# Squares of the L1 keys summed on GpSimd, self attention in packed rows, and a woven opening

## The reference, cut to what matters

```python
# layer 0, cross attention
q_in = x @ Wq + lora(x); k_in = org_ctx @ Wk + lora(org_ctx); v_in = org_ctx @ Wv + lora(org_ctx)
out = attention(q_in, k_in, v_in) + attention(q_in, ipa_ctx @ Wk_ipa, ipa_ctx @ Wv_ipa)
# layer 1, cross attention: K is normed over all 256 values of a key, before the heads are split
K = l2norm(key @ Wk + bk); V = value @ Wv + bv; Q = l2norm(query @ Wq + bq)
# layer 1, self attention: 16 heads of 16 values, 256 tokens in each of 2 batches
q = rope(x @ w_q.T); k = rope(x @ w_k.T); v = x @ w_v.T
y = softmax(q k.T / sqrt(16)) v;  return y @ w_o.T
```

## Time and profile before

| | us |
|---|---|
| median of 3 runs | 2178.71 (2175.78 to 2178.97) |
| the profiled execution | 2177.05 |
| its span, first to last instruction | 2175.3 |
| PE busy | 1946.5 (89%) |
| DVE busy | 1110.6 (51%) |
| ACT busy | 1031.1 (47%) |
| POOL busy | 627.5 (29%) |

### The profile page before, as it was taken

The page is one execution under the profiler, slowest core; times in us unless marked ns, Lnnn a source line. Parts: engine busy times, 40 slices in busy tenths (PEclk is TensorE's granted clock), DMA queues, the critical chain, the costliest instruction groups (busy, mean ns, idle before and its releaser), DMA issues. The chain is left out here.

```text
span 2175.3 us, 33966 instructions
## 1 busy us (share of the span) xinstructions
PE 1946.5 (89%) x13716; PEld 1323.1 (61%) x13716; DVE 1110.6 (51%) x1572; ACT 1031.1 (47%) x1395; POOL 627.5 (29%) x298
## 2 busy tenths in 40 slices
PE   5689999999899999999999666768998899687998
PEld 2466766667566676766666444457446644466787
DVE  2378676675666758676540543256004400465665
ACT  1144444444444444444441421036996699232443
POOL 1006555464544646555473030010000000100000
PEclk9799999999999999999999786979999999898999
DMA  5230000000300000000020100114552355200221
GB/s 183 63 112 6 6 11 6 16 6 6 93 1 15 6 6 16 6 13 4 1 77 1 58 1 1 32 49 88 85 91 61 76 94 83 78 1 1 88 88 39
DMA packets 89862, 90.60 MB, mean 42 GB/s; under 512 B 29896, under 2 KB 79760, under 8 KB 86384
## 3 DMA queue, kind: packets, MB, share of 16 engines
q1 hardware_dynamic: 86848, 85.97, 16.3%
q10 hardware_dynamic: 2864, 2.51, 0.4%
HBM read 58.57 MB, written 8.91 MB: 31 GB/s over the span
## 5 line engine op out<-in xcount | busy, mean ns | idle before, releaser
L744 POOL TENSOR_TENSOR sums<-sums,probs 128x1024 f32<-128x1024 f32 x224 | 534.8, 2388 | 355.1 <-ACT probs L777 305.4
L828 DVE TENSOR_REDUCE part_max<-psum_banks 128x2 f32<-128x1024 f32 (+1 forms) x256 | 312.6, 1224 | 125.7 <-PE psum_banks L990 121.2
L777 ACT ACTIVATE probs<-psum_banks 128x1024 f32<-128x1024 f32 x240 | 245.7, 1024 | 123.2 <-PE psum_banks L1036 116.1
L1050 PE MATMUL psum_banks<-probs,values 128*64 128x256 f32 x2048 | 278.4, 393 | 0.3 <-ACT probs L780 0.3
L755 ACT ACTIVATE keys<-psum_banks 64x512 fp32r<-64x512 f32 x256 | 151.5, 592 | 243.7 <-PE psum_banks L963 240.5
L2434 ACT ACTIVATE probs<-psum_banks,k_inv_norm 128x1024 f32<-128x1024 f32 x256 | 257.7, 1215 | 1.3 <-PE psum_banks L2449 1.2
L821 DVE TENSOR_TENSOR keys<-psum_banks,keys 64x512 fp32r<-64x512 f32 x256 | 176.3, 689 | 121.6 <-ACT keys L755 115.5
L1050 PEld LDWEIGHTS psum_banks<-probs,values 128*64 128x64 f32 x2048 | 124.5, 136 | 99.7 <-issue 60.0
L1018 PEld LDWEIGHTS psum_banks<-q_hi,keys 128*128 128x128 f32 x1024 | 138.1, 189 | 76.7 <-issue 51.7
L1018 PE MATMUL psum_banks<-q_hi,keys 128*128 128x256 f32 x1024 | 184.7, 303 | 0.0
L760 ACT ACTIVATE values<-psum_banks 128x512 f32<-128x512 f32 x128 | 76.5, 598 | 193.1 <-PE psum_banks L975 193.1
(11 more groups left out here) (436 smaller groups left out, 3159.6 us busy)
## 6 DMA issues: line engine op xcount, KB each, us to landing
k_pairs<-keys SPq DMA_DIRECT2D x192, 128.0 KB, 4.3
ctx_tok<-in_ctx SPq DMA_DIRECT2D x16, 384.0 KB, 3.4
wk_pair<-wkv_parts SPq DMA_DIRECT2D x16, 256.0 KB, 2.9
wv_quad<-wkv_parts SPq DMA_DIRECT2D x8, 512.0 KB, 3.7
w_gate_up<-in_L_ffn_gate_proj_w SPq DMA_DIRECT2D x8, 512.0 KB, 3.9
w_gate_up<-in_L_ffn_up_proj_w SPq DMA_DIRECT2D x8, 512.0 KB, 4.8
w_down<-in_L_ffn_down_proj_w SPq DMA_DIRECT2D x8, 512.0 KB, 5.7
ctx_tok_b<-in_ctx SPq DMA_DIRECT2D x8, 384.0 KB, 4.4
```

The costliest lines, as they stand in the source:

```text
L744: pool.tensor_tensor(sums[:, :, :, :], probs[:, 0, :, :, :] if step == 1 else sums[:, :, :, :], probs[:, step % SLOTS, :, :, :], ALU.add). ...
L777: act.activation(probs[:, step % SLOTS, :, :, :], scores, ACT.Exp, scale=SCALE0).then_inc(p_ready, 1)
L828: dve.tensor_reduce(part_max[:, :, i, c], psum[:, bank:bank + 2, 0:width], AX, ALU.max).then_inc(m_read, 1)
L1050: last = pe.matmul(psum[rows(h), 3, 0:L], values[:, kt, at:at + HD0], probs[:, step % SLOTS, h, j, :], start=kt == 0, stop=kt == KT - 1, t ...
```

## The change

Three parts.

1. `l1x_keys_values`: for each chunk GpSimd adds the second half of the squares to the first, and `sum_squares` has one product for each group of tokens instead of two; it waits for GpSimd's semaphore.
2. `l1_self_attention`: after the rotation q and k are split into high and low fp32r parts, which are laid out in rows of 64 (q: high, high, low, zero; k: high, low, high, one), so that two heads fill 128 rows; they are turned in four rounds of 16 transposes. First q k is computed with queries in the partitions for the maxima (16 `top` items, each a tile of queries and four heads); the negative maxima are turned (2 `turn` items) and copied by SP into the fourth row group of the queries, 8 DMAs a batch. Then k q is computed with keys in the partitions (16 `exp` items), exponentiated in one ACT instruction of 1024 elements, and weighed without a transpose of the probabilities.
3. The opening: `setup` issues the 20 weight loads before it waits for `x`; the ipa loads are issued in `l0_queries`; the ipa chain and the 8 context steps share one block; the first `wk_pair` and `wv_quad` are loaded in it.

```diff
 def setup(core, meanwhile):
                 sp.dma_start(core.x[:, :, :], ...).then_inc(x_in, 16)
+                meanwhile(sp)
                 sp.wait_ge(x_in, 16)
 def l0_queries(core, wq, xnT, qT, last, tokens):
             def _(sp):
+                for dst, src in last.pairs:
+                    sp.dma_start(dst, src).then_inc(last.arrived, 16)
                 for step in range(tokens.SLOTS):
                     tokens.start(sp, step)
+class FirstWeights:
+    def load_keys(self, sp, m):
+        sp.dma_start(self.wk_p[:, m % 2, :, :].bitcast(F32),
+                     self.w_parts[0, :, :, m % PAIRS * P:(m % PAIRS + 1) * P]).then_inc(self.wk_in[m % 2], 16)
+    def load_values(self, sp, quad): ...
+def l0_last_weights_and_context(core, last, qT, p_ipaT, parts_stored, first_w, tokens, started, cA_hi, cA_lo, cB):
+            def _(sp):
                 sp.wait_ge(parts_stored, 32)
+                first_w.load_keys(sp, 0)
+                first_w.load_values(sp, 0)
+                first_w.load_keys(sp, 1)
+                for i in range(started, STEPS_C):
+                    if i >= SLOTS:
+                        sp.wait_ge(turned, i - SLOTS + 1)
+                    tokens.start(sp, i)
+            def _(pe):
+                def turn(i):
+                    pe.wait_ge(tokens.arrived[i % SLOTS], 32 * (i // SLOTS + 1))
+                    if i >= 2:
+                        pe.wait_ge(hi_ready, 2 * (i - 1))
+                        pe.wait_ge(lo_ready, 2 * (i - 1))
+                    turn_tokens(pe, core, 2 * (i % 2), tokens.tok[:, i % SLOTS, :, :]).then_inc(turned, 1)
                 ... # transposes of the ipa tokens
+                turn(0)
                 ... # 16 products with 8 columns
+                turn(1)
+                pe.wait_ge(k_ready, 4)
                 for b in range(B):
                     ... # 8 score products of batch b
+                    turn(2 + b)
                 ... # transposes of the scores
+                for i in range(4, STEPS_C - 1):
+                    turn(i)
                 pe.wait_ge(soft, 5)
                 ... # transposes of the probabilities
+                turn(STEPS_C - 1)
+            # DVE: low(0) | 32 copies of 64x4 (16 of 64x8 before) | low(1) | each score copy, low(2 + b) |
+            #      maximum, subtraction | low(4) | sum, reciprocal, product | low(5), low(6) | p_ipaT | low(7)
+            def _(act):
+                for i in range(STEPS_C):
+                    act.wait_ge(turned, i + 1)
+                    act.activation(cA_hi[:, columns_of(i)], psum[:, 2 * (i % 2), :], ACT.Copy).then_inc(hi_ready, 1)
+                    act.activation(cB[:, columns_of(i)], psum[:, 2 * (i % 2) + 1, :], ACT.Copy).then_inc(hi_ready, 1)
+                    if i == 4:
+                        act.wait_ge(soft, 2)
+                        act.activation(e[:, :, :], s[:, :, :], ACT.Exp, scale=SCALE0).then_inc(e_ready, 1)
 def l1x_keys_values(...):
             def _(pool):
+                for c in range(CHUNKS):
+                    pool.wait_ge(squared, c * 2 + 4)
+                    pool.tensor_tensor(sq[:, 0, :], sq[:, 0, :], sq[:, 1, :], ALU.add).then_inc(sq_summed, 1)
                 def sum_squares(c, slot):
-                    pe.wait_ge(squared, c * 2 + 4)
+                    pe.wait_ge(sq_summed, c + 1)
                     pe.wait_ge(n_read, c + 1)
                     for g in range(G):
-                        for d in range(2):
-                            last = pe.matmul(psum[:, 6 + slot, g:g + 1], sq[:, d, g * P:(g + 1) * P], core.ones[:, 0:1],
-                                             start=d == 0, stop=d == 1)
+                        last = pe.matmul(psum[:, 6 + slot, g:g + 1], sq[:, 0, g * P:(g + 1) * P], core.ones[:, 0:1],
+                                         start=True, stop=True)
 def l1_self_attention(core, s):
+            rounds = [(side, first) for first in (0, HEAD_PAIRS // 2) for side in range(2)]
                 def _(pool):
+                    pool.memset(parts[:, :, 0, :, 3, :], 0.0)
+                    pool.memset(parts[:, :, 1, :, 3, 1:HD1], 0.0)
+                    pool.memset(parts[:, :, 1, :, 3, 0:1], 1.0).then_inc(padded, 1)
                     ... # per tile: qk += qk_sin, as before
                 def _(pe):
+                    for r, (side, first) in enumerate(rounds):
+                        ... # r == 1 waits rotated, v_kept; r >= 2 waits kept of round r - 2
+                        for t in range(TT):
+                            if r == 0:
+                                pe.wait_ge(hi_spread, 2 * (t + 1))
+                                pe.wait_ge(lo_ready, 2 * (t + 1))
+                            for i in range(HEAD_PAIRS // 2):
+                                last = pe.transpose(psum[:, turned_bank(r, i), t * P:(t + 1) * P], ..., core.ident[:, :])
+                        last.then_inc(turned, 1)
+                # ACT: per tile two copies of 512 elements (spread_hi), after each round two of four banks
                 def _(dve):
+                    def split(t):
+                        whole = qk[:, t, :].rearrange("p (h d) -> p h d", d=HD1)
+                        dve.wait_ge(summed, t + 1)
+                        dve.tensor_copy(qk_hi[:, t, :, :], whole).then_inc(hi_ready, 1)
+                        dve.wait_ge(hi_ready, t + 1)
+                        for side, slot in ((0, 2), (1, 1)):
+                            heads = slice(side * H1, (side + 1) * H1)
+                            dve.tensor_tensor(parts[:, t, side, :, slot, :], whole[:, heads, :], qk_hi[:, t, heads, :].bitcast(F32),
+                                              ALU.subtract).then_inc(lo_ready, 1)
+                    for t in range(TT):
+                        rotate(t)
+                        if t >= 1:
+                            split(t - 1)
+                    split(TT - 1)
+        tops = [[("top", b, t, g) for t in range(QT) for g in range(GROUPS)] for b in range(B)]
+        exps = [[("exp", b, g, k) for g in range(GROUPS) for k in range(QT)] for b in range(B)]
+        items = tops[0] + [("turn", 0)] + tops[1] + [("turn", 1)] + exps[0] + exps[1]
+            def _(sp):
+                for b in range(B):
+                    sp.wait_ge(neg_ready, b + 1)
+                    for j in range(HEAD_PAIRS):
+                        ... # one DMA of two rows of the negative maxima
+                def scores(i):
+                    if i >= SLOTS:                        # SLOTS = 3 pairs of banks
+                        other = items[i - SLOTS]
+                        pe.wait_ge(ready[other[0]], count[other])
+                    ... # turn: waits max_ready, 2 transposes; exp: waits neg_in[b]; top, exp: 4 products, 64 rows, 256 columns
+                def weigh(item):
+                    ... # waits p_ready; 4 products of 128 rows, 32 value columns, 256 columns, as in L2461
+                scores(0)
+                scores(1)
+                for i, item in enumerate(items):
+                    if i + 2 < len(items):
+                        scores(i + 2)
+                    if item[0] == "exp":
+                        weigh(item)
+                ... # 16 transposes of o_raw, then as before
```

More of the change, by code:

```diff
@@ L276, in _, with l0_queries @@
                         act.activation(out[:, 2 * c, :], raw[n][:, c, :], ACT.Copy).then_inc(hi_ready, 1)
-def l0_queries(core, wq, xnT, qT, tokens):
+def l0_queries(core, wq, xnT, qT, last, tokens):
     nc, psum = core.nc, core.psum
@@ L405, in _ @@
                                   ALU.subtract).then_inc(soft, 1)
+                low(4)
                 dve.wait_ge(e_ready, 1)
@@ new lines, in _ @@
+                    for t in range(TT):
+                        rotate(t)
+                        if t >= 1:
+                            split(t - 1)
+                    split(TT - 1)
+                    for r in range(len(rounds)):
+                        dve.wait_ge(turned, r + 1)
+                        for i in range(2, 4):
+                            dve.tensor_copy(turned_to(r, i), psum[:, turned_bank(r, i), :]).then_inc(kept[1], 1)
+        QT = L // P
+        tops = [[("top", b, t, g) for t in range(QT) for g in range(GROUPS)] for b in range(B)]
@@ new lines, in l1_self_attention @@
+        exps = [[("exp", b, g, k) for g in range(GROUPS) for k in range(QT)] for b in range(B)]
+        items = tops[0] + [("turn", 0)] + tops[1] + [("turn", 1)] + exps[0] + exps[1]
+        count = {item: sum(other[0] == item[0] for other in items[:i + 1]) for i, item in enumerate(items)}
+        probs = core.sbuf(ctx, "self_probs", [P, 4, GROUP, L])
+        neg_max = core.sbuf(ctx, "self_neg_max", [P, TT, HEAD_PAIRS, 2])
+        neg_turned = core.sbuf(ctx, "self_neg_max_turned", [H1, T], F32R)
@@ new lines, in l1_self_attention, with bank_of @@
+        ready = {"top": max_ready, "turn": neg_ready, "exp": p_ready}
+        SLOTS = 3
+        def bank_of(i):
```

(45 more changed lines are left out.)

385 lines of the change are left out of this document (179 added, 206 removed).

## The result

| | us |
|---|---|
| median after, 4 runs | 2128.12 (2123.48 to 2128.25) |
| median before, 4 runs beside them | 2178.52 (2175.78 to 2178.97) |
| ratio | 0.9766, 95% interval 0.9749 to 0.9783 |
| the profiled execution after, its span | 2128.06, 2126.4 |

The kernel is 50.4 us faster by the medians and 49.0 by the two profiled executions. Of these 49.0 the opening gave 20.7, the key norms 1.7 and the self attention 27.4; all the other stages lost 0.7 together. The forecast sum was 21.9 + 4.8 + 23.1: its total was right, and its middle term came out at a third of its size.

The account below looks back on a forecast made before the run. Stages stand one behind another, each with its own bound: loads and waits in the opening, PE in layer 1's keys. Gains 21.9+4.8+23.1 = 49.8 off 2177.05 gave 2127.3, median put at 2127.5, own range 2121 to 2134.

Parts of the forecast that it names:

- the key norms: Layer 1's key chunks: halved sum products gain 0.4 us in six chunks of each of two batches, 4.8 in all.
- (a): Opening: the 20 weight DMAs issued right behind that of `x`, so weight work starts earlier; 3.3 us gained.
- The cover of 0.5: Opening: the weights were to land 0.5 us after the moved layernorm ends, so their wait still ends last.
- (b): Opening: ipa chain and context steps woven into one block of 34 us instead of 49.43; 15.4 gained.
- The 39.2: Woven block's length in us if products with 8 columns also fall to half clock, kept in a rival.
- (c): Opening: `wk_pair` and `wv_quad` are there when the attention starts, so the first key product waits less; 3.2 us gained.
- R5: Rival, key norms: the freed 0.92 us a chunk turns into nothing, 4.8 not gained; 2132, inside the forecast's own range.
- R4: Rival, self attention: items go one behind another, 91 us instead of 36; 2183, slower than before; chance 0.02.
- R2: Rival, lower clock: self attention's exponentials at 1.73 us each, woven block 39.2; 2143, with one of the two 2133 to 2138; chance 0.17.
- R1: Rival, kinder clock and ports: splits meet no addition, rounds at full clock, woven block 30.3, exponentials at full pace; 2117; chance 0.24.

Follow-up runs that it names:

- the last kernel: The kernel after with four edits: tokens turned first, weight loads from two engines, transposes between narrow products, four copies instead of 32; 2110.78 us, ratio to before 0.9702.

## Why the prediction was right, and where it was not

**The opening**, 21.9 forecast, 20.7 measured. (a) failed by size: 1.1 for 3.3 in the two profiled executions. The landing was taken to follow the issues at the distance of before; but the earlier loads run into a full set of DMA engines (share 1.03 from 5 to 17), which the kernel with two queues shows at its limit. 1.9 was left at the weight work, and 0.8 of it went again in the queries' products, which took 17.9 to the next block instead of 17.1. A part of this shortfall is chance: over the three executions with the old opening and the nine that share the new one to there, the weight work starts 2.5 earlier (22.44 and 19.93 in the mean) and the next block too, so (a) is nearer 2.5. The first key product comes at 117.45 in the mean of the old openings and at 95.28 in the seven that are new throughout, 22.2 earlier. The cover of 0.5 over the moved layernorm became 1.5.

(b) held: 15.9 for 15.4; the narrow products took 0.16 each at full clock rather than 0.13, 5.6 in all, as the clock fell for the last of them; the scores of batch 0 took 6.43 for 6.8 and those of batch 1, at full clock, 3.67 for 5. The 39.2, with all narrow products at half clock, did not come. The prediction had put the lower clock before the scores down to these products; in the kernel before it was 0.50 from 68 on, and they began at 69.77, so there it had fallen with PE idle. The moment of the fall hardly mattered: it came 3.6 to 5.0 after the block's first transpose in the eight executions with this block, and all took 33.4 to 33.6 from there to the first key product. The clock came back at 77.8, among the scores of batch 0. That transposes alone bring it back is plainest in the self attention, where PE does nothing but the 52 transposes from 1887.20 to 1894.56:

```profile
1888.00:1890.00 2.00, 2.00 (x11) 2.00 (x10) 1.29 (x2) 1.09 (x2) 0.00 (x0) 0.50 0.00 0
1890.00:1892.00 2.00, 2.00 (x20) 2.00 (x18) 0.89 (x2) 0.89 (x2) 0.00 (x0) 0.94 0.04 8
```

The granted clock rises from 0.50 to full among them. The Trainium skill ("TensorE: Matmul & The Clock Gate", Part 4: PE-mode transpose) has it that the full clock doesn't engage for transposes; this trace disagrees.

(c) held: 3.7 for 3.2.

**The key norms**, 4.8 forecast, 1.7 measured: this is the term that was mis-sized, and R5, which put it at nothing, is closer. The bound was named rightly, DVE's low context part instead of PE. The price of the release, the time from the end of that part to PE's start, was not. PE was put 0.06 behind that part, by a row of another block where the wait is on a constant; in this loop it is 0.34, and 0.10 once the loop is written out. With 0.09 more from the chain itself (the first product after a stop takes 0.73, not 0.63) this makes 7.30 instead of 6.93 where the next chunk starts in the loop: 0.06 gained in place of 0.4. Most of the 1.7 comes from the other chunks: in the first batch the two that are followed by a product outside of the loop gained 0.29 and 0.43, near the forecast's 0.4. The addition on POOL is off the path, as argued, and doubling it costs nothing; the 0.92 that the edit frees is really there, and the order of the tokens was what kept it back.

**The self attention**, 23.1 forecast, 27.4 measured: the mechanism right, most terms somewhat dear. To the first score it was 27.5 for 29.6: three of the four splits met the additions, but lost 0.96 each rather than 1.27, and the 52 transposes took 7.36 for 8.5. After it 50.4, with the last addition itself, for 52.6: maxima every 1.14 (18.3 for 19.2), the stall between the batches 1.50 for 1.3, the one before the exponentials 2.46 for 2.1, the exponentials 17.1 for 17.5, at half clock only until 1924.5, and the end 10.6 for 11.5. R4 (items one behind another) and R2 (exponentials at half clock throughout) are not seen, and neither is R1's full clock.

The self attention gave 4.3 more than forecast, the key norms 3.1 and the opening 1.2 less, and 0.7 was lost in the other stages. That the median came out within 1 us of the forecast is luck: these errors cancelled.

## What to carry to other kernels

Before work is taken off the engine that bounds a loop, measure how long the next chain behind it is, and write down its release too: here 0.5 us of slack was all that 0.92 us of freed work could use, and 0.3 of it went into a wait inside of a loop. When such an edit brings nothing, don't take it back but move what it waits for: the same edit gave 0.9 a chunk as soon as the producers of the late operand stood first in their queues. Moving DMA issues earlier didn't bring its full distance here, with the DMA engines full: 5.4 earlier at the issue was some 2 at the landing.

## What the runs showed of the hardware

- A wait in PE's register-counted loop let the product start 0.34 behind its operand; the same wait on constants 0.10 to 0.11. Where PE had no idle time, it didn't show: with the tokens turned first the chunk was 6.44, PE's own work.
- Two DVE subtractions of 128x256 with both inputs in SBUF took 1.72 together beside one of GpSimd's additions and 0.76 without; the key chunks' DVE work, which reads PSUM, didn't notice two additions a chunk. The Trainium skill ("SBUF — State Buffer", Who interferes with whom) states an exclusive lock on the ports that the two share, and that a DVE instruction with at most one input in SBUF, outside of the two-port modes, doesn't meet it; the runs agree with both.
- The clock fell from 1.00 to 0.50 while PE was busy with products of 8 columns, at 67.5 in after and likewise in the seven other executions with such a block. It fell at 65.5 in the last kernel even with transposes between them, and in the other two kernels with such transposes 0.3 after their end. What decides the moment is open.
